# Attention and mixture-of-experts kernel: the mask row goes through the dense rows, and the key block transfers move from ScalarE's queue to SyncE's

## The reference

```python
q = (q_in @ Wq + bq).reshape(bs, q_len, h, d).transpose(0, 2, 1, 3)
k = (k_in @ Wk + bk).reshape(bs, k_len, h, d).transpose(0, 2, 1, 3)
v = (v_in @ Wv + bv).reshape(bs, k_len, h, d).transpose(0, 2, 1, 3)
score = jnp.einsum('bhqd,bhkd->bhqk', q, k) / jnp.sqrt(jnp.float32(d))
score = jnp.where(mask, jnp.float32(-1e+30), score)
attn = jax.nn.softmax(score, axis=-1)
out = jnp.einsum('bhqk,bhkd->bhqd', attn, v).transpose(0, 2, 1, 3).reshape(bs, q_len, DIM)
...
x = x + _L0_xattn_ref(_layernorm(x, axis=-1), ctx_1024, ctx_1024, mask_BxS2_bf0, L0_xattn_Wq, L0_xattn_bq, L0_xattn_Wk, L0_xattn_bk, L0_xattn_Wv, L0_xattn_bv, L0_xattn_Wo, L0_xattn_bo)
x = x + _L0_ffn_ref(_layernorm(x, axis=-1), L0_ffn_Wr, L0_ffn_W1, L0_ffn_b1, L0_ffn_W2, L0_ffn_b2)
```

## Time and profile before

| | |
|---|---|
| median of three runs | 787.57 us (782.49 to 789.75) |
| profiled execution | 786.22 us, its span 784.5 us |
| busy: PE, DVE, ACT, POOL | 80%, 71%, 69%, 63% of the span |
| packets of the DMA engines | 118,905, 164.24 MB |

### The profile page before, as it was taken

One profiled execution on the slowest core, in us unless ns is written; L12 is line 12 of the kernel. 1 busy time (PEld: TensorE's weight loads), 2 busy tenths in 40 slices (PEclk: granted clock), 3 DMA queues, 4 the chain that ended last, 5 costly groups with the idle time before them and its releaser, 6 DMA issues.

```text
span 784.5 us, 18253 instructions
## 1 busy us (share of the span) xinstructions
PE 626.8 (80%) x4964; PEld 480.8 (61%) x4964; DVE 560.7 (71%) x1813; ACT 543.2 (69%) x1060; POOL 494.1 (63%) x892
## 2 busy tenths in 40 slices
PE   1788888888888988889898527799999999999400
PEld 0465656666666666657566425688888888888300
DVE  4577788777788888887887545477777777777346
ACT  3477778777777878777777426588888888888200
POOL 8343467767576767675767763377777777677700
PEclk9999999999999999999999858899999999999855
DMA  4766777668577877676764246887787777774088
GB/s 140 221 193 188 228 218 222 184 210 241 162 208 226 242 227 200 207 218 193 182 209 126 82 127 216 264 253 244 242 253 244 249 239 253 236 244 139 1 294 348
DMA packets 118905, 164.24 MB, mean 209 GB/s; under 512 B 22479, under 2 KB 77286, under 8 KB 118823
## 3 DMA queue, kind: packets, MB, share of 16 engines
q1 hardware_dynamic: 88711, 126.14, 51.9%
q10 hardware_dynamic: 21024, 20.06, 9.5%
q0 software_dynamic: 9088, 17.07, 6.7%
HBM read 73.07 MB, written 33.92 MB: 136 GB/s over the span
## 4 chain that ended last, share of the span: by engine, by line
PE 48%; DMA 21%; issue 10%; ACT 7%; POOL 7%; SPq 4%; DVE 3%; ACTq 1%; POOLq 0%; DVEq 0%
DMA kb<-dense 12%; PE bank L1281 6%; PE bank L1254 5%; PE bank L1434 4%; PE bank L1432 4%; PE bank L1417 4%; PE bank L1420 4%; PE bank L1418 4%; PE bank L1433 4%; PE bank L1266 4%; DMA qb<-negm 3%; DMA qb<-yd 3%; POOL xd L538 2%; PE bank L1394 2%; PE bank L1242 2%
## 5 line engine op out<-in xcount | busy, mean ns | idle before, releaser
L638 POOL DMA_INDIRECT yd<-vs,idt x156 | 165.1, 1058 | 87.4 <-DVE vs L950 48.9
L695 DVE TENSOR_REDUCE mx<-bank 128x4 f32<-128x480 f32 x256 | 160.0, 650 | 47.9 <-PE bank L1254 47.4
L538 POOL DMA_INDIRECT xd<-rows,posi x128 | 128.9, 1007 | 88.4 <-DVE posi L801 58.6
L998 ACT ACTIVATE pt<-bank,mcol 120x512 f32<-120x512 f32 x256 | 171.6, 691 | 13.5 <-PE bank L1266 6.7
L936 DVE TENSOR_TENSOR qb<-hid,qb 128x512 fp32r<-128x512 f32 x156 | 109.7, 703 | 73.5 <-ACT hid L1148 72.4
L1145 ACT ACTIVATE qb<-bank,btile 128x512 fp32r<-128x512 f32 x156 | 107.6, 690 | 37.5 <-PE bank L1434 29.8
L1254 PE MATMUL bank<-kb,dense 128*128 128x480 f32 x256 | 87.5, 424 | 40.9 <-DMA kb<-dense 35.1
L1266 PE MATMUL bank<-qb,dense 128*120 128x512 f32 x256 | 100.5, 459 | 13.9 <-DMA qb<-negm 7.8
L1148 ACT ACTIVATE hid<-bank,btile 128x512 f32<-128x512 f32 x156 | 106.3, 681 | 0.0
L1030 ACT ACTIVATE ots<-bank 128x512 f32<-128x512 f32 x64 | 38.2, 597 | 69.5 <-PE bank L1281 69.5
L1254 PEld LDWEIGHTS bank<-kb,dense 128*128 128x128 f32 x256 | 46.1, 199 | 62.2 <-DMA kb<-dense 48.2
(11 more groups left out here) (169 smaller groups left out, 1515.4 us busy)
## 6 DMA issues: line engine op xcount, KB each, us to landing
kb<-wd SPq DMA_DIRECT2D x40, 512.0 KB, 5.2
qb<-wd SPq DMA_DIRECT2D x38, 512.0 KB, 5.0
qb<-dense SPq DMA_DIRECT2D x128, 128.0 KB
dense<-comp SPq DMA_DIRECT2D x64, 248.0 KB, 2.4
kb<-dense ACTq DMA_DIRECT2D x128, 120.0 KB, 3.5
rows<-xd SPq DMA_DIRECT2D x39, 264.0 KB, 2.8
wd<-wsp SPq DMA_DIRECT2D x16, 512.0 KB, 3.8
qb<-yd SPq DMA_DIRECT2D x16, 512.0 KB, 6.1
```

What stands on the lines that cost most here:

```text
L538: g.indirect_dma_start(xd, bass.IndirectOffsetOnAxis(ap=posi[r % 4][:, bk:bk + 1], axis=0), rows[r % 4][:, bk // 2, bk % 2, :], None, boun ...
L638: g.indirect_dma_start(yd, bass.IndirectOffsetOnAxis(ap=idt[k][:, j:j + 1], axis=0), yrow[p.parity][:, j, :], None, bounds_check=2 * NTOK ...
L695: v.tensor_reduce(mx[c % 2][:, :, gg, b], wide[m % 2][:, 0:J * KL].rearrange("p (j k) -> p j k", j=J), op=ALU.max, axis=AX.X).then_inc(w_f ...
L998: a.activation(pt[i % NP][:].rearrange("p j q -> p (j q)"), scores[t % 2][0:KL, :], ACT.Exp, bias=mcol[:, 2 * c + t // G:2 * c + t // G + ...
```

## The change

The mask row moves from row 11 to row 31 of each group of 32. It is no longer written over the key blocks but into the key half of the dense tile, in the four partitions 31, 63, 95 and 127, one slot earlier (in slot n for chunk n+3, ahead of the high spreads). From there the key block transfers carry it along. In the query half these four partitions hold ones, which a small reduce on DVE prepares (`mask_q`). Since row 31 of the query blocks must stay zero, the query block transfers carry 31 rows instead of 32. `kfirst` goes; all four key block transfers count on `kblk`. They are issued by SP, right behind the query blocks of the slot, and wait additionally for the mask row.

```diff
-    NHI, NLO, MSK = 3, 7, 11
+    NHI, NLO, MSK = 3, 7, 31
...
+        mask_q = sb("mask_q", [P, 1])
...
-        mask_row = two("mask_row")
+        mask_row = four("mask_row")
...
             def mask_rows(c):
 
+                if c < ND:
+                    sp.wait_ge(dense_set, 2 * (c + 1))
+                else:
+                    sp.wait_ge(b_full, 8 * (c - ND + 1))
                 if c == 0:
                     sp.wait_ge(mask_dram, 16)
-                sp.wait_ge(kfirst[c % 2], 16 * (c // 2 + 1))
-                sp.dma_start(kb[c % 2][MSK:MSK + 1].rearrange("a j g n -> a (j g) n").bitcast(F32),
-                             maskd.bitcast(F32)[2 * c:2 * c + 2, :].rearrange("(a g b) k -> a g (b k)", a=1, g=1).to_broadcast([1, G * J, K2])).then_inc(mask_row[c % 2], 16)
+                sp.dma_start(dense[c % ND][MSK::R, :, N2:NK].bitcast(F32),
+                             maskd.bitcast(F32)[2 * c:2 * c + 2, :].rearrange("(a g b) k -> a g (b k)", a=1, g=1).to_broadcast([J, G, K2])).then_inc(mask_row[c % ND], 16)
...
                 for j in range(J):
-                    sp.dma_start(qb[c % 2][R * j:R * j + R, j, :, :].bitcast(F32),
-                                 dense[c % ND][R * j:R * j + R, :, 0:N2].bitcast(F32)).then_inc(qblk[c % 2], 16)
+                    sp.dma_start(qb[c % 2][R * j:R * j + R - 1, j, :, :].bitcast(F32),
+                                 dense[c % ND][R * j:R * j + R - 1, :, 0:N2].bitcast(F32)).then_inc(qblk[c % 2], 16)
+
+            def key_block(c, j):
+
+                if not chunk(c):
+                    return
+                if j == 0:
+                    if c < 2:
+                        sp.wait_ge(kb_zero, c + 1)
+                    else:
+                        sp.wait_ge(w_full, 8 * (c - 1))
+                    sp.wait_ge(dn_in[c % 2], 64 * (c // 2 + 1))
+                    sp.wait_ge(mask_row[c % ND], 16 * (c // ND + 1))
+                sp.dma_start(kb[c % 2][R * j:R * j + R, j, :, :].bitcast(F32),
+                             dense[c % ND][R * j:R * j + R, :, N2:NK].bitcast(F32)).then_inc(kblk[c % 2], 16)
...
             def slot(n):
                 if chunk(n + 1):
                     query_blocks(n + 1)
-                if chunk(n + 2):
-                    mask_rows(n + 2)
+                for j in range(J):
+                    key_block(n + 2, j)
...
                 if chunk(n + 3):
+                    mask_rows(n + 3)
                     spread_high(n + 3)
...
-                g.tensor_copy(dense[k][:, :, 0:N2], ident[:, MSK:MSK + 1].rearrange("p (g a) -> p g a", g=1).to_broadcast([P, G, N2])).then_inc(dense_set, 1)
+                g.tensor_copy(dense[k][:, :, 0:N2], mask_q[:, :].rearrange("p (g a) -> p g a", g=1).to_broadcast([P, G, N2])).then_inc(dense_set, 1)
...
+            v.tensor_reduce(mask_q[:, :], ident[:, MSK::R], op=ALU.add, axis=AX.X).then_inc(pad_set, 1)
...
-                key_block(n + 2, 0)
                 if chunk(n - 1):
                     take_heads(2 * n - 1)
-                key_block(n + 2, 1)
...
-                key_block(n + 2, 2)
 
                 exponential(n, 2)
-                key_block(n + 2, 3)
...
                 if u == 0:
-                    pe.wait_ge(kblk[c % 2], 48 * (c // 2 + 1))
-                    pe.wait_ge(mask_row[c % 2], 16 * (c // 2 + 1))
+                    pe.wait_ge(kblk[c % 2], 64 * (c // 2 + 1))
```

More of the change, by code:

```diff
@@ L211, in moe_attention @@
         w_full, w_free = sem("w_full"), sem("w_free")
-        dn_in, qblk, kblk, kfirst, mrow = two("dn_in"), two("qblk"), two("kblk"), two("kfirst"), two("mrow")
+        dn_in, qblk, kblk, mrow = two("dn_in"), two("qblk"), two("kblk"), two("mrow")
         v_full, v_taken = sem("v_full"), sem("v_taken")
@@ L565, in _ @@
             pool.wait_ge(half_done, 1)
-            pool.wait_ge(pad_set, 1)
+            pool.wait_ge(pad_set, 2)
             pads(0)
@@ L1060, in top_exps @@
                 a.activation(tope[:].rearrange("p b e -> p (b e)"), topd[:].rearrange("p b e -> p (b e)"), ACT.Exp).then_inc(top_exp, 1)
[L1062 to L1073, removed]
             def take_rows(r):
```

## The result

The changed kernel takes 1392.72 us (median of four, 1390.59 to 1394.84) against 785.03 for the kernel before in the same session: a ratio of 1.775 (95% interval 1.761 to 1.789). It is 77% slower. The prediction was 1371 us, range 1200 to 1500.

What follows compares the result with a forecast made beforehand. No engine was full; transfers bound attention. Query blocks on one engine (23.6 us, plus 4.9 and 2.4) make a 30.9 us period instead of 12.7: 786 + 564 + 21 = 1371 us, range 1200 to 1500.

Steps and rivals of the forecast that it cites:

- One engine for 31 rows: Query block transfers: 31 rows have no divisor but themselves and 1, so each goes through one DMA engine instead of sixteen.
- one missing semaphore packet: SP's queue: 9,615 extra packets instead of 9,616; the 120-row `maskuT` went out in 15 equal parts.
- The drain: A chunk's query blocks, 507,904 B in 496 packets on one engine at 21.5 GB/s, take 23.6 us.
- SP is held: SP's issues stall while one engine drains, moving 0 to 4.8 us of later work behind it; 2.4 us taken.
- rival (a): Query blocks on one engine but SP not held: period 28.5 us, 1297 us in all; chance 0.28.
- the sum: Whole kernel: 786 us plus 564 for 31 slots of 30.9 instead of 12.7 us, plus 21 for chunk 0: 1371.
- 4.9 + 2.4 us: Between two chunks' query block transfers: 4.9 us for landing, maxima, spreads and half a store; 2.4 for held SP issues.
- What is late next: SP's slot: maxima wait for query blocks to land, then spreads, then next query blocks; period at least 28.5, taken 30.9 us.
- The other work has room in it: PE in a slot: needs 10.8 us, or 21.5 at half clock, within the 30.9 us period.
- Rival (b): Query block transfers still spread over sixteen or four engines; SP's wait and PE's 35.1 us go: 751 us; chance 0.13.
- 7.1 us of cover: Query blocks cost nothing up to 7.1 us: maxima come 9.2 us after the first issue, less 2.1 for a small transfer.
- SP's load: SP's issues per slot grow from 7.7 to 10.1 of 12.7 us; 2.6 us left, and the 2.1 of waits fit.

## Why the prediction was right

**One engine for 31 rows: right.** The step from one missing semaphore packet to a cut into equal shares of whole rows gave the packet count of the kernel after exactly. 32 rows take the loss away, and 16 + 15 rows all but 112 us of it, with the packets of 16 and 15 engines. The rule that the Trainium skill states ("DMA: Bandwidth & Descriptors", section "Why a DMA increments its semaphore by 16 and not by 1") gives the same: the largest number up to 16 that divides the slowest dimension. The runs agree with it: 6.6% of sixteen engines' time while such transfers drain.

**The drain: right in size, by two errors.** Taken at 21.5 GB/s, 23.6 us. The engine moves 24 GB/s while it is alone, a packet each 42 ns, which would be 20.9 us. But in the slot shown the query blocks' packets run from 1.4 to 24.5 us after the first issue, 23.1 us. The two middle transfers take 5.4 and 5.3 us each, the first 6.4 and the last 6.1; POOL's rows move during the first and key blocks during the last, but what slows the packets there wasn't tested. That the two errors cancel is luck.

**SP is held: right.** Not at the first two issues (0.75 and 0.69 us), then for 6.5, 5.5 and 4.9 us. The rival (a) without that falls. But the 2.4 us that the sum added for it weren't paid where it put them: the issues behind the query blocks are through at 523.96, before the query blocks have landed and the maxima are issued (526.50). How many packets the queue takes before it holds SP wasn't measured.

**What closes the slot: wrong.** The prediction put 4.9 + 2.4 us between two chunks' transfers, with the maxima as the gate, 500 us of PE's waiting on `qb<-negm`, and SP's longest wait ahead of the maxima. PE's wait for the maxima is 18.5 us and the one for key blocks 586; SP waits 77.6 us ahead of the maxima, but 102.5 for the by-key products. The step that failed is "What is late next": it followed SP's queue and missed that the key blocks stand behind the query blocks on the same engine, and that PE has the by-query products, which need them, ahead of the last by-key products, which free the buffer for the next query blocks. The true gap is 8.6 us in that slot: 1.4 from issue to first packet, 1.3 for the key blocks' packets on that engine, 0.5 until PE starts on them, 5.4 of PE. A slot is 31.8 us instead of 30.9. That 8.6 lies near 7.3 is luck too, since of the prediction's terms only the 2.1 us from issue to landing is among the true ones (1.4 + 0.5).

**"The other work has room in it": wrong for PE.** PE has idle time, but a piece of it lies in the circle, and with the lower clock that follows upon its idle time the piece takes 5.4 us instead of 3.05. From the second slot on it takes 4.6 to 5.5 us, 5.2 on average; against 3.05, one slot of another run, that is an estimate of some 64 us of the 606 lost.

**The sum.** 31 x (31.84 - 12.72) = 593 us, where 564 stood. The time from the first query block issue of chunk 31 to the end grew from 364.4 to 378.1 us, 13.7, where 21 stood. 593 + 13.7 = 606.6, the difference of the spans. The prediction was 22 us low, a small miss for a gate that it had wrong.

**Rival (b)'s price: wrong.** It gave 751 us and 7.1 us of cover. With 32 rows the time is 781, with 5.2 us of drain in one transfer it is 913. The 751 rests on key blocks that land earlier, so that PE's wait goes: it stayed (39.4 us), because in one queue they come behind the query blocks. The 7.1 rests on the maxima as what slow query blocks delay: they delay the key blocks behind them first. The working on SP's load holds: no wait of SP grew into a bound with 32 rows.

## What to carry to other kernels

Look at the row count of a transfer before its bytes: leaving out one row of 32 made it as narrow as one DMA engine, at 24 GB/s. Where a row must not be copied, copying it and making it harmless, or cutting the transfer into two counts that divide, can cost far less: 781 and 902 us here. (The run with 32 rows leaves out the step that makes the row harmless: a mask that is set anywhere would be added twice.) Before a wait is removed from a queue, list what stands behind it: here those were transfers that then ran beside the ones that the next stage was waiting for. And when a transfer becomes slow, follow the circle through the consuming engine's program order back to the buffer's release, not only the issuing queue.

## What was not expected of the hardware

A queue holds its issuer when much lies on one engine: issues of 0.6 us became 6.9 us, and issues of key blocks, most of whose packets then went over idle engines, were held with them (up to 5.3 us). On the one busy engine two queues take turns packet by packet: 82 ns between two query block packets with ACT's key blocks in between (31 rows in the kernel before), 42 without. And a slower slot made PE slower as well: PE sat idle in every slot, the granted clock over the attention part fell from 0.97 to 0.69, and the same 3,512 products cost 58 us more busy time.
